# Weight dequantisation rescheduled around a seven-product matmul: a second float buffer, sum chains moved on GpSimd, code bits built through PSUM

## The reference

```
def dequant_nvfp4(W_packed, scales, block=32):   # W_packed [N, K/2], two codes per byte
    low, high = W_packed & 15, W_packed >> 4 & 15
    vals = NVFP4_LUT[stack([low, high], -1).reshape(N, -1)]   # 0 .5 1 1.5 2 3 4 6 and their negatives
    return (vals.reshape(N, K // block, block) * scales[:, :, None]).reshape(N, K)

gate = dequant(gate_W_packed, gate_scales)       # 4096 x 512
up   = dequant(up_W_packed, up_scales)           # 4096 x 512
down = dequant(down_W_packed, down_scales)       # 512 x 4096
y = x + (gelu(x2 @ gate.T) * (x2 @ up.T)) @ down.T     # in outline, x2 the normed tokens, 2048 of them
```

## Time and profile before

| | |
|---|---|
| median of three runs | 1183.62 us |
| the profiled execution's own time | 1182.23 us |
| its span | 1180.5 us |
| PE busy | 1125.7 us (95%) |
| DVE, POOL, ACT busy | 873.4, 664.4, 490.9 us |
| mean granted TensorE clock | 0.996 |
| pairs 8 to 63 | 325.9 to 1167.3 us of the span |

### The profile page before, as it was taken

How to read it: one execution, slowest core, us unless ns; L and a number is a source line. 1 busy time by engine, 2 the same in 40 slices (tenths; PEclk the granted TensorE clock), 3 DMA queues, 4 the chain that set the end, 5 groups by cost and what they waited for, 6 DMA issues and landing times.

```text
span 1180.5 us, 22307 instructions
## 1 busy us (share of the span) xinstructions
PE 1125.7 (95%) x8842; PEld 861.3 (73%) x8842; DVE 873.4 (74%) x1537; ACT 490.9 (42%) x1148; POOL 664.4 (56%) x665
## 2 busy tenths in 40 slices
PE   9999999999999998899989998999899989998999
PEld 5566655665476676778877886788678877887886
DVE  7788665477777655788868887878787868886664
ACT  4433343353344443344444444444444444444432
POOL 2386534165966753666476556755675666566320
PEclk9999999999999999999999999999999999999999
DMA  8021101000111322222232222222223222321221
GB/s 295 1 73 46 36 29 36 10 10 27 63 30 61 108 90 107 90 90 108 90 108 91 108 90 96 102 108 90 90 108 108 90 90 90 114 97 69 77 76 72
DMA packets 30232, 96.65 MB, mean 82 GB/s; under 512 B 3440, under 2 KB 3760, under 8 KB 23472
## 3 DMA queue, kind: packets, MB, share of 16 engines
q1 hardware_dynamic: 30128, 95.23, 22.7%
HBM read 63.73 MB, written 31.49 MB: 81 GB/s over the span
## 4 chain that ended last, share of the span: by engine, by line
PE 63%; DVE 18%; POOL 7%; issue 5%; DMA 4%; ACT 2%; SPq 0%; DVEq 0%; POOLq 0%; ACTq 0%
PE ps L621 25%; PE ps L690 10%; PE ps L451 8%; PE ps L582 7%; PE ps L730 6%; DMA load<-scales 4%; DVE fw L1273 3%; DVE X L1321 2%; DVE X L1318 2%; DVE bigB L1377 2%; DVE X L1319 2%; PE ps L417 1%; DVE bigC L1360 1%; DVE load L1377 1%; PE ps L543 1%
## 5 line engine op out<-in xcount | busy, mean ns | idle before, releaser
L621 PE MATMUL ps<-REG,WR 128*128 128x256 f16 x1344 | 183.4, 273 | 2.1 <-ACT load L1013 2.1
L621 PE MATMUL ps<-XT,WR 128*128 128x256 f16 x1344 | 183.3, 273 | 0.0
L1013 ACT COPY load<-ps 128x256 f32<-128x256 f32 x168 | 62.4, 371 | 231.6 <-PE ps L621 230.9
L621 PEld LDWEIGHTS ps<-REG,WR 128*128 128x128 f16 x1344 | 129.7, 98 | 24.5 <-ACT load L1013 3.9
L621 PEld LDWEIGHTS ps<-XT,WR 128*128 128x128 f16 x1344 | 131.5, 98 | 15.4
L1377 DVE TENSOR_TENSOR load<-load,ps 128x256 f32<-128x256 f32 x168 | 69.6, 415 | 75.4 <-PE ps L621 59.0
L1308 DVE SCALAR_TENSOR_TENSOR X<-ps,X 128x512 f32<-128x512 f32 x161 | 108.4, 685 | 21.6 <-PE ps L690 19.2
L1377 DVE TENSOR_TENSOR bigB<-bigB,ps 128x256 f32<-128x256 f32 x168 | 69.8, 415 | 70.1 <-ACT bigB L1013 59.3
L1013 ACT COPY bigB<-ps 128x256 f32<-128x256 f32 x168 | 62.6, 373 | 120.3 <-PE ps L621 120.2
L621 PE MATMUL ps<-REG,bigA 128*128 128x256 f16 x672 | 93.1, 275 | 15.1 <-ACT bigB L1013 15.1
L690 PE MATMUL ps<-WR,ihl_s 128*128 128x256 f16 x684 | 90.7, 274 | 5.2 <-DVE X L1294 3.4
(11 more groups left out here) (215 smaller groups left out, 2548.0 us busy)
## 6 DMA issues: line engine op xcount, KB each, us to landing
kept<-X SPq DMA_DIRECT2D x26, 1024.0 KB, 4.0
X<-kept SPq DMA_DIRECT2D x26, 1024.0 KB, 4.8
load<-codes SPq DMA_DIRECT2D x48, 256.0 KB
load<-scales SPq DMA_DIRECT2D x48, 256.0 KB
bigA<-cla SPq DMA_DIRECT2D x14, 256.0 KB, 3.2
X<-x SPq DMA_DIRECT2D x3, 1024.0 KB, 13.2
WR<-wqkv SPq DMA_DIRECT2D x2, 1024.0 KB, 9.9
y<-X SPq DMA_DIRECT2D x2, 1024.0 KB, 4.8
```

The lines of the kernel that those rows point to most:

```text
L621: mm = eng.matmul(half_bank(kind, name), w(wp, kt), x(xp, kt), start=(first and n == 0), stop=(n == 5), skip_group_check=True)
L1013: eng.copy(start, half_bank(kind, name)).then_inc(s_snap, 1)
```

## The change

**VectorE.** The four integer operations are other ones and are no longer split over the pair: multiply the codes by 4097 into PSUM, shift and mask from PSUM into `load` (sign), shift and mask from PSUM to PSUM (magnitude), and an or. They stand in one block behind the two `into_rows`, and `combine("gate", m, "C12")` is moved behind it. For m >= 10 chunk k's bits are built in the pair before the one in which it is finished, and `dq_finish` always stands behind the gate's C11. Chunks are finished at c = 2, 3, 5, 6, 7, 0 (before: 2, 3, 5, 6, 0, 0), so the block of bits stands in c = 1, 2, 4, 5, 6, 7.

**A second float buffer.** First chunks go alternately to `wf` and to a part of `X1`; before, a first chunk waited until the couple before it had been split.

**ScalarE and GpSimd.** ScalarE's `dequant` stands behind the gelu of the odd tile in every pair but c = 7. GpSimd works on "e", "o", "T01" and "T23" of the pair before in one piece, and the sum chain behind them, at most some three operations of it in a pair.

SP's program and PE's are unchanged, but for the new `finished_in`. The core of the diff:

```diff
 def finished_in(k):
 
-    g, c = k // 6, k % 6
-    if k < 12:
-        return k - 2
-    return 8 * g + (-6, -5, -3, -2, 0, 0)[c]
+    return k - 2 if k < 12 else 8 * (k // 6) + (-6, -5, -3, -2, -1, 0)[k % 6]
+
+
+FINISHED = {finished_in(k): k for k in range(10, 48)}
...
+        wfs = [wf[:, :, :], two(E3[:, 1024:2048])]
+        def floats(k):
+
+            return wfs[pair_count(k) % 2 if k >= 12 else 0]
...
# ScalarE, in the loop over m
-                if summed and m % 8 == 1:
-                    dequant(summed)
...
                 gelu(oo, half_bank("gate", "P4"))
                 if summed:
                     dq_sums(summed, 0, 2)
-                if m % 8 == 0 and m > 8:
-                    dequant(6 * g + 4)
...
+                elif m >= 10 and m in FINISHED:
+                    dequant(FINISHED[m])
                 snapshot("up", m, "P1")
...
# VectorE
             def dq_bits(k):
-                dq_magnitude(k)
-                dq_sign(k)
-
-            def dq_magnitude(k):
-                s = place(k)
+
+                s, codes_ = place(k), codes_in(k)
                 dv.wait_ge(s_chunk[s], loaded(k))
-                eng.scalar_tensor_tensor(raw[s], raw[s], 12, raw[s], ALU.logical_shift_left,
-                                         ALU.bitwise_or).then_inc(s_dq, 1)
-                dv.wait_ge(s_dq, 6 * k + 1)
...
-                eng.tensor_scalar(codes_in(k), raw[s], 9, 0x0E000E00, ALU.logical_shift_left,
+                eng.tensor_scalar(codes_, raw[s], 4097, None, ALU.mult).then_inc(s_dq, 1)
+                dv.wait_ge(s_dq, 6 * k + 1)
+                eng.tensor_scalar(raw[s], codes_, 12, -0x7FFF8000, ALU.logical_shift_left,
                                   ALU.bitwise_and).then_inc(s_dq, 1)
...
                 combine("gate", m, "C11")
-                if steady and c in (5, 6):
-                    dq_finish(6 * g + c + 3)
-                if c == 0 and m > 8:
-                    dq_finish(6 * g + 4)
-                if bits:
-                    dq_magnitude(bits)
+                if m == 10:
+                    dq_bits(12)
+                if m >= 10 and m in FINISHED:
+                    dq_finish(FINISHED[m])
                 combine("gate", m, "C22")
+                if n in SEVEN:
+                    for name in (("P1", "P2"), ("P3", "P7"))[m % 2]:
+                        into_rows(n, name)
+                else:
+                    gather(n, 2 * m % 4)
...
+                if m < 10:
+                    dq_bits(FINISHED[m])
+                elif m + 1 in FINISHED:
+                    dq_bits(FINISHED[m + 1])
                 combine("gate", m, "C12")
-                if n in SEVEN:
-                    for name in (("P1", "P2"), ("P3", "P7"))[m % 2]:
-                        into_rows(n, name)
...
                 combine("up", m, "C11")
...
# GpSimd
                 if m - 1 in SEVEN_PAIRS:
-                    operands_low(m - 1, ("e", "o"))
+                    operands_low(m - 1, ("e", "o", "T01", "T23"))
...
-                if summed and m % 8 == 1:
-                    dequant(summed)
-                    dq_last_sum(summed)
-                if m - 1 in SEVEN_PAIRS:
-                    operands_low(m - 1, ("T01", "T23"))
                 if summed:
+                    if c != 7:
+                        dq_last_sum(summed)
                     dq_sums(summed)
...
+                if k and not second(k):
                     dequant(k)
-                    dq_difference(k + 1)
+                    if c in (2, 5):
+                        dq_difference(k + 1)
+                elif k and k > 11:
+                    if c == 0:
+                        dq_difference(k)
+                    dq_first_sums(k)
+                    dequant(k)
+                    if c == 6:
+                        dq_last_sum(k)
```

More of the change, by code:

```diff
@@ L238, in sides @@
             return ap.bitcast(F16).rearrange("p (a k n) -> p a k n", a=2, k=2)
-        WDX = [[sides(E3[:, 512 * j:512 * j + 512]) for j in range(3)],
+        wfs = [wf[:, :, :], two(E3[:, 1024:2048])]
+        WDX = [[sides(E3[:, 0:512]), sides(E3[:, 512:1024]), XT[:, :, 0:2, 1792:2048]],
                [sides(E2[:, 1024:1536]), sides(E2[:, 1536:2048]), sides(tb[:, :])]]
@@ L940, in dq_mul @@
                         ac.wait_ge(*downs_done(g - 2))
-                    eng.copy(buf[:, 0, 2 * (k % 6) + nib, :], wf[:, nib, :]).then_inc(s_whi, 1)
+                    eng.copy(buf[:, 0, 2 * (k % 6) + nib, :], floats(k)[:, nib, :]).then_inc(s_whi, 1)
             def dq_first(k):
@@ L955, in dq_first @@
                     ac.wait_ge(s_tlo, 16)
-                eng.copy(tiles(buf[:, 0, base:base + 2, :], 0), tiles(wf[:, :, :], 0)).then_inc(s_whi, 1)
+                eng.copy(tiles(buf[:, 0, base:base + 2, :], 0), tiles(floats(k), 0)).then_inc(s_whi, 1)
             def dq_second(k):
@@ L1337, in dq_magnitude @@
                         dv.wait_ge(sm7, value)
-                eng.tensor_scalar(codes_in(k), raw[s], 9, 0x0E000E00, ALU.logical_shift_left,
+                eng.tensor_scalar(codes_, raw[s], 4097, None, ALU.mult).then_inc(s_dq, 1)
+                dv.wait_ge(s_dq, 6 * k + 1)
+                eng.tensor_scalar(raw[s], codes_, 12, -0x7FFF8000, ALU.logical_shift_left,
                                   ALU.bitwise_and).then_inc(s_dq, 1)
-            def dq_sign(k):
-                s = place(k)
-                eng.tensor_scalar(raw[s], raw[s], 12, -0x7FFF8000, ALU.logical_shift_left,
+                dv.wait_ge(s_dq, 6 * k + 2)
+                eng.tensor_scalar(codes_, codes_, 9, 0x0E000E00, ALU.logical_shift_left,
                                   ALU.bitwise_and).then_inc(s_dq, 1)
                 dv.wait_ge(s_dq, 6 * k + 3)
-                eng.tensor_tensor(codes_in(k), codes_in(k), raw[s], ALU.bitwise_or).then_inc(s_dq, 1)
+                eng.tensor_tensor(codes_, codes_, raw[s], ALU.bitwise_or).then_inc(s_dq, 1)
             def dq_finish(k):
-                s, dst = place(k), wf2 if second(k) else wf
+                s, dst = place(k), wf2 if second(k) else floats(k)
                 dv.wait_ge(s_dq, 6 * k + 4)
@@ L1357, in dq_finish @@
                 for nib in range(2):
-                    if k and not second(k) and not second(k - 1):
+                    if 0 < k < 12 and not second(k) and not second(k - 1):
                         dv.wait_ge(s_wlo, WLO[k - 1][nib])
@@ L1480, in _ @@
                     rows_of_second(m - 1)
[L1481 to L1484, removed]
+                done = pair_base("up", m, 3)
                 combine("gate", m, "C11")
-                if steady and c in (5, 6):
-                    dq_finish(6 * g + c + 3)
-                if c == 0 and m > 8:
-                    dq_finish(6 * g + 4)
-                if bits:
-                    dq_magnitude(bits)
-                combine("gate", m, "C22")
-                if m in (9, 11):
-                    token_sums(m // 2 - 2, 0, 2)
-                if m in (10, 12):
-                    token_sums(m // 2 - 3, 2, 4)
-                if bits and c == 3:
-                    dq_sign(bits)
-                combine("gate", m, "C12")
+                if m == 10:
+                    dq_bits(12)
+                if m >= 10 and m in FINISHED:
+                    dq_finish(FINISHED[m])
+                combine("gate", m, "C22")
                 if n in SEVEN:
@@ L1504, in _ @@
                     gather(n, 2 * m % 4)
-                if bits and c == 3:
-                    dq_finish(bits)
-                elif bits:
-                    dq_sign(bits)
+                if m in (9, 11):
+                    token_sums(m // 2 - 2, 0, 2)
+                if m in (10, 12):
+                    token_sums(m // 2 - 3, 2, 4)
+                if m < 10:
+                    dq_bits(FINISHED[m])
+                elif m + 1 in FINISHED:
+                    dq_bits(FINISHED[m + 1])
+                combine("gate", m, "C12")
                 combine("up", m, "C11")
-                if bits and (m < 10 or c == 2):
-                    dq_finish(bits)
+                if m < 10:
+                    dq_finish(FINISHED[m])
                 if n in SEVEN and m % 2 == 0:
                     into_rows(n, "P5")
-                if steady and c == 5:
-                    dq_magnitude(6 * g + 9)
-                if c == 0 and m > 8:
-                    dq_magnitude(6 * g + 5)
                 combine("up", m, "C22")
@@ L1533, in _ @@
                     operand_sums(m)
-                if c == 0 and m > 8:
-                    dq_finish(6 * g + 5)
             rows_of_second(NI // 2 - 1)
@@ L1659, in dq_last_sum @@
             def dq_last_sum(k):
-                a11, a12 = tiles(wf[:, :, :], 0), tiles(wf2, 0)
+                a11, a12 = tiles(floats(k), 0), tiles(wf2, 0)
                 pl.wait_ge(s_chain, 4 * (pair_count(k) - 1) + 3)
```

54 lines of the change are left out of this document (21 added, 33 removed).

## The result

The changed kernel takes 1287.81 us, the median of four runs (1286.35 to 1288.39), against 1183.79 for the kernel before: a ratio of 1.088 [1.0861, 1.0899]. The forecast was 1287. The profiled execution has a span of 1284.6 us, 104.1 more than before, and a mean granted clock of 0.955 (0.996 before).

What follows compares the result with a forecast made beforehand. PE's matmuls and its waits, about 10.4 us of stalls a group, bound the kernel. A group came to 110.1 + 0.3 + 21.5 + 6.8 = 138.7 against 120.5; +107 in all gave 1290.5, put at 1287 us (1238 to 1325).

Steps and rivals of the forecast that it cites:

- The sum: Groups of eight pairs: 138.7 us against 120.5 in each group from 24 to 55; all groups together +107 us.
- The stalls: PE waits ahead of up's P7 in six pairs of a group, behind the bits and C12: 21.5 us a group.
- B: Time into the pair when the bits' first operation starts: 10.4 us in m = 37, 12.1 behind a fill.
- The clock: TensorE at its lower clock behind each gap at c = 2, 5, 6, 7: 1.7 us each, 6.8 a group.
- The chain: GpSimd's sum chain ahead of the operands' low parts stalls PE; moving it removes at most 10.4 us a group.
- `dq_finish` ahead of C22: On VectorE in six pairs it keeps a little of the old stalls: 0.3 us a group (0 to 1).
- by the row the edit costs nothing: VectorE's moved shift: 0.70 us through PSUM against a mean of 0.727 from `load` to `load`, so no cost.
- The load isn't awaited where I say: Rival: the next chunk lands before VectorE needs it, stalls are 6.3 us a group: 1157 us, chance 0.07.
- tipping point: B at 8.5 in four pairs, about 10.4 us of stall a group, decides between faster and slower.
- All stalls go: Rival: up's snapshot doesn't wait for C12 in time, 10.4 us a group are gone: some 1125 us, chance 0.03.
- The clock stays up: Rival: TensorE's clock falls at most now and then, so 37 us drop out: 1250 us, chance 0.22.

Runs made afterwards that it cites:

- D: The changed kernel with 34 (odd pairs) or 42 (even) unused matmuls ahead of up's P7 in pairs 18 to 55 with c = 2, 5, 6, 7: 1250.26 us.
- C: The changed kernel with the bits directly behind C12 and, from chunk 13 on, the codes loaded one pair earlier on their own semaphore: 1121.29 us.
- E: C with GpSimd's difference and first sums of the second chunks put back ahead of the operands' low parts: 1213.88 us.
- F: B with the four operations on the bits as before the change, shift-or and sign shift from `load` to `load`: 1168.62 us.
- B: The changed kernel with codes loaded one pair earlier from chunk 13 on, scales on their own semaphore, bits still ahead of C12: 1158.93 us.
- G: The kernel before with only the form of the four operations on the bits changed, at their old places: 1186.57 us.

## Why the prediction was right

- *The sum.* 138.7 a group, four times: 137.0, 136.5, 139.0, 140.5, mean 138.25. Group 16 to 23: 144.1, measured 143.4. Group 8 to 15: 138.2 and 139.3. Group 56 to 63: 110.6 and 110.0. All groups together 947.7 forecast, 945.7 measured.
- *The stalls.* In the groups 24 to 55 P7 started late by 0.95 us (c = 1; forecast 1.2), 0.5 (c = 4; 0.9), 3.9 to 4.4 (c = 5; 4.2), 4.6 to 5.1 (c = 7; 4.8), 5.0 to 6.5 (c = 2; 5.2) and 4.5 to 5.1 (c = 6; 5.2). The mean sum of 20.9 stands against 21.5; errors of both signs cancel in it. PE's waits on the copy are 35, up to 7.2 us long, where the prediction named some 22 of 4 to 5: the long ones came where it said, and short ones in other pairs beside them. In m = 37 and 34 B was 10.3 and 12.0 for 10.4 and 12.1: the two durations taken from the trace of before, 4.3 from the issue to the use and 7.6 behind a fill, came back as 4.2 and 7.2.
- *The clock.* 37 us forecast for 22 gaps, which is 34 for the 20 that D fills; D gives 35.5 to 37.5. Per group 6.8 against 138.25 less 131.25 (the mean of D's four groups 24 to 55: 131.9, 130.7, 130.7, 131.7) = 7.0. The price of 1.7 us was right with some luck. It was read from pair 25 alone, and in the kernel before the next pair gave most of it back: 16.0 us in m = 26 against 17.4 in m = 34, groups of 120.6 and 120.3. One stretch a gap holds as a mean only (last section). The last step, from the sum's 1290.5 to 1287, was a judgement and not a reading.
- *The chain.* The upper bound, all 10.4 us of a group, was right: once the other delays are taken out (C), nothing is left. By E the chain ahead of "e" costs 16.2 us in the group 40 to 47 of the new order, clock included. That it was the cause of all 10.4 in the old one isn't shown, and the trace of before speaks against it. PE's largest wait there in total isn't for the copy into `bigB` (15.1 us):

```profile
PE ps L621 <- DVE load L1377: 15.7, 14, 1.4
```

  This is P3's wait for the gate's C22: 0.93, 1.40 and 0.81 us in m = 42, 44 and 46, of the 8.2 us of the group 40 to 47 in which PE does nothing. In m = 38, with the same wait of 0.81, GpSimd stood idle for 6.1 us before "e"; VectorE worked from the pair's start to C22 with no wait above 0.1 us, with two operations on the bits (0.42 and 0.70 us) and `dq_finish` (1.28) ahead of it. So what C gained over the kernel before belongs to the rescheduling as a whole, VectorE's part with it.
- *`dq_finish` ahead of C22.* Forecast 0.3 a group; C has 0.1.
- *What was off.* The step "by the row the edit costs nothing" for the new form of the operations. It compared the moved shift alone, by its mean of 727 ns, and that mean hides two prices. From pair 8 on the shift takes 0.42 us in the 19 chunks where GpSimd is idle meanwhile, and 0.65 to 1.43 us in the 19 where it works. I left out the shift-or, which the change removes: 789 ns in the mean before, 1015 at the new place (F), beside GpSimd's work. The new form saves 9.7 us ahead of C12 (F against B) and costs 3.7 at the old places (G). The Trainium skill's "VectorE: DVE Perf Modes", section "Why PSUM operands drop a tier", rules out the double rate for an operand in PSUM; the estimate from it was 0.35 us a chunk. The trace agrees where GpSimd is idle: 0.42 us in SBUF against 0.69 in PSUM, a gain of 0.27 us that F doesn't get, since from pair 16 on GpSimd works beside each of its shifts (0.66 to 0.78 us).
- *The rivals.* "The load isn't awaited where I say", 1157, is B's 1158.9. Its tipping point (B = 8.5) isn't contradicted, but no run comes near it: with B at 7.6 the kernel is faster than before, at 10.3 and 12 slower. "All stalls go", 1125, is C's 1121.3. "The clock stays up", 1250, is near D's 1250.3, though D fills 20 of the 22 gaps. Each was close to the price of a state that the change didn't reach.

## What to carry to other kernels

An in-order engine's wait for a load delays everything behind it, so a step that begins with such a wait belongs behind what the bottleneck waits for, however short the step itself is; here 2.8 us of work carried a wait of 3.6 us in the mean (85.9 us in 24 waits) to the critical path. When a buffer has two readers, load its halves on two semaphores, each half as soon as its own reader is done: that alone was worth 129 us of 1288 here. And a rearrangement that is bad as a whole may hold a good one: with the block moved and the loads split, the same change is 62 us faster than the kernel before.

## What the runs showed of the hardware

**VectorE and GpSimd hold each other up on SBUF.** An addition of 128x256 float32 with both operands in SBUF took 1.38 us where GpSimd's "e" began beside it, and 0.42 us in E, where GpSimd stood idle at that place (m = 38; VectorE from the changed kernel's m = 37, then from E):

```profile
826.44 1.38 DVE L1317 TENSOR_TENSOR X<-fw,X 128x256 f32<-128x256 f32 x1
```
```profile
797.66 0.42 DVE L1317 TENSOR_TENSOR X<-fw,X 128x256 f32<-128x256 f32 x1
```

The shift-or of F is the same thing (0.68 alone, 0.73 to 1.65 beside GpSimd, from pair 8 on), and so is the one-operand shift from `load` to `load` in the kernel before (0.42 us alone, 0.65 to 1.43 beside GpSimd). The four operations on the bits that read or write PSUM showed nothing of it: from pair 8 on, all four lie between 0.67 and 0.70 us in B. A mean over a group hides which of the two prices will be paid at a new place.

**A longer gap can leave the clock alone where a shorter one costs it.** The window behind P7 in m = 37, after a gap of 3.88 us, is at full clock:

```profile
837.90:841.40 3.50, 2.85 (x26) 2.50 (x27) 1.52 (x5) 0.97 (x3) 0.00 (x0) 1.00 0.00 0
```

In m = 45 the gap is shorter, 3.73 us, and the matmuls fall to half rate 1.3 us behind its end (twelve in 1.3 us, then six in 1.46):

```profile
975.24 0.83 PE L626 MATMUL ps<-REG,bigA 128*128 128x256 f16 x6 [3.73 <-ACT bigB L1019]
...
976.56 1.46 PE L626 MATMUL ps<-REG,WR 128*128 128x256 f16 x6
```

The pairs with c = 5 took 18.9 us (m = 29, gap 4.22), 17.15 (m = 37, 3.88) and 18.2 (m = 45, 3.73). The changed kernel has 22 stretches at the lower clock, 116.1 us in all, and of the 20 long gaps from m = 18 on only that of m = 37 has none with it. The mean price of these gaps by D, 1.8 to 1.9 us, is near the forecast 1.7, though the price of a single one could not be foretold from its length.
